# One graph layer's gate products on split operands, and one buffer for the adjacency's rows

## The reference

```
h = relu(bn(conv1(x^T)));  h = bn(conv2(h), 17 taps, pad 8);  x_conv = relu(h + x^T)^T
s = x @ w_se.T;  dist = |s_n - s_m|^2;  A = exp(-dist) * adj
msg = relu(x @ w_msg.T + b_msg);  x_nmp = A @ msg
gi = concat[x_conv, x_nmp] @ w_ih.T + b_ih;   gh = x @ w_hh.T + b_hh      # 3 gates of 128
r = sigmoid(gi_r + gh_r);  z = sigmoid(gi_z + gh_z);  n = tanh(gi_n + r * gh_n)
out = x_in + (1 - z) * n + z * x          # x = layernorm(x_in)
```

## Time and profile before

| what | value |
|---|---|
| median of 3 runs | 3378.24 us (3372.72 to 3381.37) |
| the profiled execution | 3367.48 us, its span 3365.7 us |
| PE busy in the whole span | 2615.8 us, 78% |
| DVE busy | 2233.8 us, 66% |
| ACT busy | 1726.5 us, 51% |
| POOL busy | 872.9 us, 26% |
| the changed layer in the span | from 32.3 us (first conv1) to about 516 us (last gate), then the routing's end |
| its 15 distances from turn to turn | 26.8 to 32.7 us, and 45.6 us for turn 2 |

### The profile page before, as it was taken

How to read it: one execution, slowest core, us unless ns; L and a number is a source line. 1 busy time by engine, 2 the same in 40 slices (tenths; PEclk the granted TensorE clock), 3 DMA queues, 4 the chain that set the end, 5 groups by cost and what they waited for, 6 DMA issues and landing times. The chain is left out here.

```text
span 3365.7 us, 67707 instructions
## 1 busy us (share of the span) xinstructions
PE 2615.8 (78%) x19578; PEld 2098.6 (62%) x19578; DVE 2233.8 (66%) x6587; ACT 1726.5 (51%) x5002; POOL 872.9 (26%) x863
## 2 busy tenths in 40 slices
PE   5799995787177675078999998799987777669992
PEld 4566674777177575065787787466654444468882
DVE  5667664444667455767888886699986666644445
ACT  2233333444367353275656653677756666435554
POOL 0232233444335343230001010000001343434332
PEclk9899997889688797589999999899998888779996
DMA  5111112222332121320000000100001000012125
GB/s 199 38 57 52 44 45 57 64 62 61 126 121 69 50 55 53 115 84 1 1 1 0 0 1 3 33 19 25 19 20 52 20 24 21 25 54 56 52 56 169
DMA packets 142570, 168.84 MB, mean 50 GB/s; under 512 B 19920, under 2 KB 118224, under 8 KB 141776
## 3 DMA queue, kind: packets, MB, share of 16 engines
q1 hardware_dynamic: 116688, 118.67, 11.8%
q0 software_dynamic: 21504, 44.74, 3.9%
q10 hardware_dynamic: 4224, 3.59, 0.4%
HBM read 115.87 MB, written 51.05 MB: 50 GB/s over the span
## 5 line engine op out<-in xcount | busy, mean ns | idle before, releaser
L1221 POOL DMA_INDIRECT y_rows<-ffn_e_rows_out,ffn_e_scatter_at x352 | 338.9, 963 | 522.4 <-DVE ffn_e_rows_out L1249 328.3
L1363 PE MATMUL bank<-ffn_e_xT,ffn_e_mine 128*128 128x128 f32 x3360 | 453.0, 283 | 26.6 <-DVE ffn_e_hid L1269 12.2
L1363 PEld LDWEIGHTS bank<-ffn_e_xT,ffn_e_mine 128*128 128x128 f32 x3360 | 420.1, 199 | 34.4 <-issue 30.2
L744 POOL DMA_INDIRECT sorted_rows<-ffn_rows,ffn_slot x320 | 316.0, 987 | 230.5 <-issue 219.4
L1269 DVE TENSOR_TENSOR ffn_e_hid<-ffn_e_act,bank 128x256 f32<-128x256 f32 (+1 forms) x280 | 135.9, 485 | 270.1 <-ACT ffn_e_act L1323 212.2
L1297 ACT ACTIVATE ffn_e_mine<-constants 128x512 f32 (+1 forms) x352 | 250.3, 712 | 96.4 <-issue 85.1
L1373 PE MATMUL bank<-ffn_e_mine,ffn_e_hid 128*128 128x128 f32 x1968 | 290.8, 283 | 11.1 <-DVE ffn_e_hid L1269 7.0
L1373 PEld LDWEIGHTS bank<-ffn_e_mine,ffn_e_hid 128*128 128x128 f32 x1968 | 258.0, 198 | 16.7 <-DVE ffn_e_hid L1269 9.6
L2702 ACT ACTIVATE gnn_prob<-bank,gnn_low 128x256 f32<-128x256 f32 x512 | 203.1, 500 | 107.7 <-DVE gnn_low L2616 107.7
L1323 ACT ACTIVATE ffn_e_act<-bank 128x256 f32<-128x256 f32 (+1 forms) x280 | 120.5, 430 | 243.1 <-PE bank L1363 200.4
L1257 DVE TENSOR_SCALAR ffn_e_mine<-constants 128x256 f32 (+2 forms) x352 | 127.7, 364 | 127.8 <-PE bank L1373 78.1
(11 more groups left out here) (509 smaller groups left out, 6378.5 us busy)
## 6 DMA issues: line engine op xcount, KB each, us to landing
g_adj<-in_adjT SPq DMA_DIRECT2D x48, 512.0 KB, 3.9
ffn_e_rows_in<-sorted_rows SPq DMA_DIRECT2D x346, 66.0 KB
ffn_c_y<-y_rows SPq DMA_DIRECT2D x80, 256.0 KB, 3.1
g_adj_rows<-in_adj SPq DMA_DIRECT2D x16, 512.0 KB
gnn_adj<-in_adjT SPq DMA_DIRECT2D x16, 512.0 KB, 3.8
constants<-in_ffn SPq DMA_DIRECT2D x1, 6281.0 KB, 22.4
y_rows<-ffn_e_rows_out,ffn_e_scatter_at POOLq DMA_INDIRECT x352
constants<-in_ffn SPq DMA_DIRECT2D x1, 5204.0 KB, 16.3
```

The source lines that it names most:

```text
L744: eng.indirect_dma_start(c.sorted_rows, bass.IndirectOffsetOnAxis(r.slot[par][:, k, j:j + 1], 0), r.rows[par][:, j, :], None).then_inc(r.d ...
L1221: g.indirect_dma_start(c.y_rows, bass.IndirectOffsetOnAxis(scatter_at[par][:, k:k + 1], 0), rows_out[par][:, k, :], None).then_inc(scatter ...
L1363: ins = pe.matmul(chunk(part, ch), chunk(weights[:, i * HALF:(i + 1) * HALF], ch), x, start=True, stop=True)
```

## The change

Ten float32 products of 512 columns per turn become three float32r products each: the four that read `hT` (conv1, gates r, z, n; weights `own_hi`, `own_lo`) and the six that read `xconv` and `nmp` (weights `gate_hi`, `gate_lo`). The weights are split once at the start on VectorE. In every turn ScalarE makes `hT_hi`, `xconv_hi` and `nmp_hi`, and VectorE the three remainders `hT_lo`, `xconv_lo` and `nmp_lo`; `nmp` in full is no longer made. TensorE now takes xconv's products ahead of nmp's. To find the room, several buffers move into weights that are dead after the split, and the rows of the adjacency have one buffer in place of two, so that their transfer waits for the sum of the turn before.

```diff
-        adj_rows = [sb(f"adj_rows{i}", [P, 4, NODES]) for i in range(2)]
-        msg = sb("msg", [P, TT, D])
-        nmp = sb("nmp", [P, TURN])
-        ghb, q, e, outT = (sb(n, [P, TURN]) for n in ("ghb", "q", "e", "outT"))
+        A = differ_or_A[:, 0:4 * NODES].rearrange("p (m n) -> p m n", m=4)
+        adj_rows = sb("adj_rows", [P, 4, NODES])
+        msg = w["w_ih"][:, 0:TURN].rearrange("p (k d) -> p k d", k=TT)
+        ghb, q, e, outT = (w["conv2"][:, i * TURN:(i + 1) * TURN] for i in range(4))
...
-                    if not first and not (isinstance(t, int) and t == 1):
-                        sp.wait_ge(degrees_done, t - 1)
-                    sp.dma_start(adj_rows[par][:], c.adj[t]).then_inc(adj_rows_ready[par], 16)
+                    if not first:
+                        sp.wait_ge(degrees_done, t)
+                    sp.dma_start(adj_rows[:], c.adj[t]).then_inc(adj_rows_ready, 16)
...
                 normalise(v, c, 0, h).then_inc(h_ready, 1)
+                v.tensor_copy(gate_hi[:], w_ih)
+                v.tensor_copy(own_hi[:, 0:3, :], w_hh)
+                v.tensor_copy(own_hi[:, 3, :], w["conv1"]).then_inc(gates_split, 1)
+                v.wait_ge(gates_split, 1)
+                v.tensor_tensor(gate_lo[:], w_ih, gate_hi[:], ALU.subtract)
+                v.tensor_tensor(own_lo[:, 0:3, :], w_hh, own_hi[:, 0:3, :], ALU.subtract)
+                v.tensor_tensor(own_lo[:, 3, :], w["conv1"], own_hi[:, 3, :], ALU.subtract).then_inc(gates_split, 1)
...
                     if not first:
                         route.vector_first(v, t - 1, 1 - par, before)
+                    v.wait_ge(xconv_ready, t + 1)
+                    if not first:
+                        v.wait_ge(z_ps, t)
+                    v.tensor_tensor(xconv_lo[:], xconv[:], xconv_hi[:], ALU.subtract).then_inc(xconv_lo_ready, 1)
+                    if not last:
+                        v.wait_ge(hT_hi_ready, t + 2)
+                        if not first:
+                            v.wait_ge(r_ps, t)
+                        v.tensor_tensor(hT_lo[1 - par][:], hT[1 - par][:], hT_hi[1 - par][:], ALU.subtract).then_inc(hT_lo_ready, 1)
+                    if not first:
                         route.vector_second(v, t - 1, before)
+                    v.wait_ge(nmp_hi_ready, t + 1)
+                    v.tensor_tensor(nmp_lo[:], B[3][:], nmp_hi[:], ALU.subtract).then_inc(nmp_lo_ready, 1)
+                    if not first:
                         route.vector_chosen(v, t - 1, before)
...
+                    a.activation(xconv_hi[:].rearrange(by_parity, two=2), both_rows, ACT.Relu, bias=shift2).then_inc(xconv_hi_ready, 1)
+                    a.activation(xconv[:].rearrange(by_parity, two=2), both_rows, ACT.Relu, bias=shift2).then_inc(xconv_ready, 1)
                     a.wait_ge(nmp_ps, t + 1)
...
+                    a.activation(nmp_hi[:], B[3][:], ACT.Copy).then_inc(nmp_hi_ready, 1)
...
-                    mm(B[1][:], w["conv1"], hTp[:], start=True, stop=True).then_inc(c1_ps, 1)
+                    def own(out, at, start=True, stop=True):
+                        mm(out, own_hi[:, at, :], hT_hi[par][:], start=start, stop=False)
+                        mm(out, own_lo[:, at, :], hT_hi[par][:], start=False, stop=False)
+                        return mm(out, own_hi[:, at, :], hT_lo[par][:], start=False, stop=stop)
...
-                    pe.wait_ge(xconv_ready, t + 1)
+                    pe.wait_ge(nmp_lo_ready, t + 1)
                     for gate, done in ((0, r_ps), (2, n_ps), (1, z_ps)):
-                        mm(B[5 + gate][:], w_ih[:, 0, gate, :], xconv[:], start=False, stop=True).then_inc(done, 1)
+                        mm(B[5 + gate][:], gate_hi[:, 1, gate, :], nmp_lo[:], start=False, stop=True).then_inc(done, 1)
```

More of the change, by code:

```diff
@@ L267, in phase_gnn0 @@
         taps_hi, taps_lo = (sbr(n, [P, ALL_TAPS, D]) for n in ("taps_hi", "taps_lo"))
-        differ = sb("differ", [P, EVEN, D])
+        differ_or_A = sb("differ_or_A", [P, EVEN * D])
+        differ = differ_or_A[:].rearrange("p (k d) -> p k d", k=EVEN)
         uv_hi, uv_lo = (sbr(n, [P, 2, 2, SEG]) for n in ("uv_hi", "uv_lo"))
@@ L299, in phase_gnn0 @@
         adj_ready = [sem(f"adj_ready{i}") for i in range(2)]
-        adj_rows_ready = [sem(f"adj_rows_ready{i}") for i in range(2)]
+        adj_rows_ready = sem("adj_rows_ready")
         degrees_done = sem("degrees_done")
@@ L502, in evac_hT @@
                     a.activation(hT[par][:], B[0][:], ACT.Copy).then_inc(hT_ready, 1)
+                    if not (isinstance(t, int) and t < 2):
+                        a.wait_ge(hT_lo_ready, t - 1)
+                    a.activation(hT_hi[par][:], B[0][:], ACT.Copy).then_inc(hT_hi_ready, 1)
                 a.wait_ge(consts, 2)
@@ L544, in turn @@
                         evac_hT(t + 1, 1 - par)
+                    a.wait_ge(xpre_ready, t + 1)
+                    if not first:
+                        a.wait_ge(z_ps, t)
+                        a.wait_ge(xconv_lo_ready, t)
+                    both_rows = q[:].rearrange("p (two n) -> p two n", two=2)
+                    a.activation(xconv_hi[:].rearrange(by_parity, two=2), both_rows, ACT.Relu, bias=shift2).then_inc(xconv_hi_ready, 1)
+                    a.activation(xconv[:].rearrange(by_parity, two=2), both_rows, ACT.Relu, bias=shift2).then_inc(xconv_ready, 1)
                     a.wait_ge(nmp_ps, t + 1)
-                    a.activation(nmp[:], B[3][:], ACT.Copy).then_inc(nmp_ready, 1)
-                    a.wait_ge(xpre_ready, t + 1)
-                    a.activation(xconv[:].rearrange(by_parity, two=2), q[:].rearrange("p (two n) -> p two n", two=2), ACT.Relu, bias=shift2).then_inc(xconv_ready, 1)
+                    if not first:
+                        a.wait_ge(nmp_lo_ready, t)
+                    a.activation(nmp_hi[:], B[3][:], ACT.Copy).then_inc(nmp_hi_ready, 1)
                     if not first:
@@ L573, in to_tokens @@
                     pe.wait_ge(outT_ready, t + 1)
+                    pe.wait_ge(hT_hi_ready, t + 2 if not (isinstance(t, int) and t == TURNS - 1) else TURNS)
                     for k in range(TT):
@@ L616, in turn @@
                     pe.wait_ge(s_ready, t + 1)
-                    mm(B[4][:], w_hh[:, 2, :], hTp[:], start=True, stop=True).then_inc(ghn_ps, 1)
+                    own(B[4][:], 2).then_inc(ghn_ps, 1)
                     pe.wait_ge(s2_ready, t + 1)
@@ L648, in turn @@
                     for gate in range(2):
-                        mm(B[5 + gate][:], w_hh[:, gate, :], hTp[:], start=True, stop=False)
-                    pe.wait_ge(nmp_ready, t + 1)
-                    for gate in range(3):
-                        mm(B[5 + gate][:], w_ih[:, 1, gate, :], nmp[:], start=(gate == 2), stop=False)
-                    pe.wait_ge(xconv_ready, t + 1)
+                        own(B[5 + gate][:], gate, stop=False)
+                    pe.wait_ge(xconv_hi_ready, t + 1)
+                    for weights in (gate_hi, gate_lo):
+                        for gate in range(3):
+                            mm(B[5 + gate][:], weights[:, 0, gate, :], xconv_hi[:], start=(gate == 2 and weights is gate_hi), stop=False)
+                    pe.wait_ge(xconv_lo_ready, t + 1)
+                    for gate in range(3):
+                        mm(B[5 + gate][:], gate_hi[:, 0, gate, :], xconv_lo[:], start=False, stop=False)
+                    pe.wait_ge(nmp_hi_ready, t + 1)
+                    for weights in (gate_hi, gate_lo):
+                        for gate in range(3):
+                            mm(B[5 + gate][:], weights[:, 1, gate, :], nmp_hi[:], start=False, stop=False)
+                    pe.wait_ge(nmp_lo_ready, t + 1)
                     for gate, done in ((0, r_ps), (2, n_ps), (1, z_ps)):
-                        mm(B[5 + gate][:], w_ih[:, 0, gate, :], xconv[:], start=False, stop=True).then_inc(done, 1)
+                        mm(B[5 + gate][:], gate_hi[:, 1, gate, :], nmp_lo[:], start=False, stop=True).then_inc(done, 1)
                 every_turn(pe, turn)
```

23 lines of the change are left out of this document (17 added, 6 removed).

## The result

| | kernel before | changed kernel |
|---|---|---|
| median (lowest to highest, 4 runs each) | 3376.67 us (3372.72 to 3381.37) | 3416.69 us (3412.68 to 3421.02) |
| profiled execution, its span | 3367.48, 3365.7 us | 3421.02, 3419.2 us |

The changed kernel takes 1.0116 times as long (95% interval 1.0100 to 1.0133), 40 us more. The prediction was 3405 us, with a range of 3360 to 3430.

The account below looks back on a forecast made before the run. It took a circle through VectorE's chain and TensorE's late signals to bound the loop; 13.8 + 1.5 + 2.8 + 2.5 + 0 + 6 = 26.6 us on the median of 3378.2 gave 3405 us, range 3360 to 3430.

Parts of the forecast that it names:

- T: Arrival of the router's logits at VectorE in each turn; 21.9 us after msg's L420, predicted to stay so.
- constants' wait: VectorE in turn 0 waits for the next layer's constants, issued later behind turn 1's rows: +6 us (+3.5 to +9).
- 11 loop turns: Loop turns from 131.5 to 458.3 us: each 31.0 us against 29.7, +13.8 us in all.
- turn 13 to 14: One of the last turns, between logits' arrivals at 458.3 and 486.36: 29.6 us against 28.1, +1.5.
- turn 14 to 15: Last distance between logits' arrivals, 486.36 to 511.35: 27.8 us against 25.0, +2.8.
- last T to e: After the last logits' arrival, L471 comes at 6.15 us in place of 3.7: +2.5.
- The circle through VectorE and the late signals: Loop turn: VectorE's work sets when transfers begin, TensorE's signals among them come late; 21.9 + 6.15 + 2.9 = 31.0 us.
- One sign of the prediction: In the turn after the change, TensorE should idle before L702 and L709, about 0.8 us before nmp_lo.
- T to e: VectorE's routing chain from the logits' arrival to L471, with three subtractions added: 6.15 us, before 3.5.
- rival C: TensorE's clock halves at the last pass and each turn's first 2.6 us: +32 us, 3437 us; chance 0.08.
- e to msg: From L471 to the next turn's L420 on VectorE: 2.9 us after the change, 3.3 before.
- Rival A: TensorE is the loop's bound, late signals only the profile's reading: -28 us, 3350 us; chance 0.09.

Follow-up runs that it names:

- h3: Changed kernel, constants' transfer moved ahead, three remainders before the logits' wait, logits held until the indirect transfers end; 3410.87 us, ratio to kernel before 0.9993.
- h4: Changed kernel, logits held until the indirect transfers end, own products of gates r and z made four times over; 3433.72 us, ratio to kernel before 1.0060.
- e5: Changed kernel run again unchanged, on a chip where signals come at once; 3104.82 us, ratio to kernel before 0.9978.
- e8: Changed kernel, constants' transfer ahead, three remainders before the logits' wait, indirect transfers held until gate r is done; 3343.61 us, ratio to kernel before 0.9919.
- e4: Kernel before with only the single buffer for the adjacency's rows, signals at once; 3117.99 us, ratio to kernel before 1.0009.

## Why the prediction was right, and where its steps were off

Term by term, from the starts of T in the profiled execution of each:

| step | predicted | measured |
|---|---|---|
| constants' wait | +6 | wait of 4.66; T of turn 2 is 4.4 later |
| 11 loop turns | +13.8 | 356.0 - 326.8 = +29.2 |
| turn 13 to 14 | +1.5 | 32.0 against 28.1: +3.9 |
| turn 14 to 15 | +2.8 | 30.3 against 25.0: +5.3 |
| last T to e | +2.5 | 7.0 against 3.7: +3.3 |
| sum | +26.6 | +46 |

The two profiled executions differ by 53.5 us, of which 46 are in this sum; the other 7 lie elsewhere, and what they are was not tried. The medians differ by 40: the profiled execution of the changed kernel lies 4.3 us above its median, that of the kernel before 9.2 below.

**What held.** The circle through VectorE and the late signals bounds the loop on the chip of the result: 21.9 us from msg to T before and after, nmp_lo at T + 4.9 (predicted 5.0), TensorE idle for xconv_lo, the constants issued at 50.6 us. TensorE's savings brought nothing there, and h3 shows, on another chip with late signals, that undoing the place of the subtractions and of the constants undoes the loss. One sign of the prediction didn't come: TensorE is not idle before L709 in any loop turn, since its passes ahead of it end after nmp_lo is there.

**What was mis-sized.** The circle came to 32.4 us in place of 31.0. First, **T to e** took 7.3 us on average in place of 6.15. The sum had TensorE ready when nmp_lo is there. But behind its wait of 4 us the clock fell (0.50, that is 1.2 in place of 2.4 GHz, in the passes that follow), and its nine passes after xconv_lo ended late. That is a mild form of rival C, which the prediction priced at another place (the turn's start) and gave 0.08; it should have stood in the sum. h4 measures it: 6.15 with the gap filled. The rule of the Trainium skill that stood beside rival C ("TensorE: Matmul & The Clock Gate", section Why this matters for your kernels) warned of just such a gap, and the trace agrees: 4.55 us idle, then 0.43 us per pass. The trace of before had it too. The prediction held the loop's clock of 0.98 against C, with gaps of 1.4 us, but that is a mean: in three of the loop's turns the clock fell to 0.50 behind a gap of 2.1 us, and the longest turn before (32.5 us, T at 397.64), which the prediction put down to nmp, is one of them:

```profile
393.93 1.43 PE L1015 MATMUL bank<-constants,ffn_r_hT 128*128 128x16 f32 x8 [2.11 <-ACT ffn_r_hT L982]
395.20 3.76 PE L649 MATMUL bank<-g_hT,constants 128*128 128x512 f32 x4
398.75 4.01 PE L652 MATMUL bank<-g_nmp,constants 128*128 128x512 f32 x6
```

Second, **e to msg** took 3.17 for 2.9. Where the clock stays up through the passes ahead of it, it takes 2.94 (e5) and 3.03 (h4), so most of this too goes with the clock. Third, a float32r pass takes 0.23 us, not the 0.215 that was taken, nearer the upper bound of 0.242. It costs nothing here and 0.4 us per turn where TensorE is the bound (1.7 saved, not 2.1). The last turns took more for the same first two reasons, and because T comes 1.1 and 0.7 us later after msg (21.6 and 19.4 for 20.5 and 18.75); what sets that was not tried.

**What stood on one chip.** Rival A, at 0.09, is what happens on the two chips where signals come at once: ratio 0.9978. Nothing in the trace of before could tell that the lateness differs from chip to chip, and a single profile has only one chip. The forecast is right for a chip with late signals, and that the result was measured on one was luck, which the chances didn't price. As a statement on the kernel it isn't general.

## What to carry to other kernels

Before work is put into a chain, find out where in the turn its engine waits, and whether the inputs of the new work are there by then: where signals come late, the three subtractions behind the logits (with the constants' transfer behind a wait) cost 21 us more than ahead of them, and where TensorE is the bound, their place makes 0.3 us of a turn. An engine that is made to wait a few microseconds may come back at half its clock, and that belongs in the sum. A mean clock near 1 over a loop can hide turns at half the clock: read it turn by turn. Where a signal comes late by the trace, look for what another engine issues at that time, and move that; and compare two chips before a bound is called the kernel's.

## What the runs showed of the hardware

The same kernel took 3111 and 3112 us on two chips and 3371 to 3414 us on the others. Within the changed layer the difference is in when TensorE's signals get through while GpSimd issues indirect transfers: VectorE waits 5.7 us for logits whose matmuls ended long before ("remote"), against 0.5 us (released by the logits' matmul) on the other chips with the same transfers of 0.96 us in flight. The late signals follow the transfers when these are moved (e8).

This layer accounts for a small part only: its last T comes 30 us earlier in e4 (501.66) than in the kernel before (531.17), of 245 us between their spans (3120.4 and 3365.7). The rest fits the same cause. In each of the fourteen traces GpSimd issues 672 indirect transfers and has one long stretch without any, and that stretch takes 1292 to 1297 us on every chip. All of the 245 us lie in the time outside it: 2074 us before, 1824 in e4. That late signals make the difference in the later stages too was not traced step by step.

Why some chips have it stays open. Each chip was seen once, so whether the lateness belongs to the chip or to its state at the time isn't shown either.
